# TensorE's first two steps ahead of its loop, the order check on ScalarE, and other orders in the front and the tail of a graph layer

## What is computed

```python
x = x + layer(relu(layernorm(x)), edge_attr_48)

def layer(nodes, edges):
    agg = segment_sum(edges, dst, num_segments=12500)
    u = graph_globals[batch]                  # batch is all 0
    h = concatenate([nodes, agg, u], axis=1)
    return relu(h @ W1 + b1) @ W2 + b2        # W1: 240x256, W2: 256x128
```

## Time and profile before

| | before |
|---|---|
| median of 3 runs (lowest, highest) | 264.44 us (264.34, 265.47) |
| the profiled execution: its time | 264.3 us |
| its span in the profile | 262.5 us |
| mean granted clock of TensorE | 0.978 |
| TensorE busy | 241.3 us, 92% |
| VectorE busy | 229.8 us, 88% |
| ScalarE busy | 144.2 us, 55% |
| POOL busy | 104.9 us, 40% |
| moved by DMA | 94.49 MB, mean 360 GB/s |

### The profile page before, as it was taken

The page is one execution under the profiler, slowest core; times in us unless marked ns, Lnnn a source line. Parts: engine busy times, 40 slices in busy tenths (PEclk is TensorE's granted clock), DMA queues, the critical chain, the costliest instruction groups (busy, mean ns, idle before and its releaser), DMA issues.

```text
span 262.5 us, 17352 instructions
## 1 busy us (share of the span) xinstructions
PE 241.3 (92%) x7438; PEld 197.2 (75%) x7438; DVE 229.8 (88%) x555; ACT 144.2 (55%) x315; POOL 104.9 (40%) x113
## 2 busy tenths in 40 slices
PE   6719799999898999999999999999999999999994
PEld 3517677878777877877987887887897788789753
DVE  2899978999999999999999999999899999997362
...
GB/s 238 372 373 282 391 348 353 379 367 367 345 376 346 332 385 367 355 375 381 382 382 380 381 370 385 373 370 377 376 363 363 368 369 379 382 379 363 403 402 118
DMA packets 70874, 94.49 MB, mean 360 GB/s; under 512 B 4324, under 2 KB 64260, under 8 KB 70854
## 3 DMA queue, kind: packets, MB, share of 16 engines
...
q10 hardware_dynamic: 956, 0.00, 0.2%
...
q0 software_dynamic: 96, 0.00, 0.0%
...
## 4 chain that ended last, share of the span: by engine, by line
PE 59%; DVE 15%; DMA 15%; issue 7%; ACT 3%; DVEq 1%; ACTq 0%
PE group_bank L1063 21%; DMA edge_buf<-in_edge_attr 13%; PE out_bank L1129 12%; PE hidden_bank L1112 10%; PE window_bank L1085 5%; DVE onehot L816 4%; PE out_bank L1102 4%; PE hidden_bank L1116 3%; PE hidden_bank L1118 3%; ACT agg L679 2%; DVE bn L861 2%; DVE out_own L770 2%; DVE agg L845 2%; DVE placing L828 1%; DMA dst_rows<-in_dst 1%
## 5 line engine op out<-in xcount | busy, mean ns | idle before, releaser
L816 DVE TENSOR_TENSOR onehot<-rel,const_bank 128x896 f32<-128x896 f32 (+1 forms) x122 | 122.9, 1023 | 6.1 <-issue 6.0
L1063 PE MATMUL group_bank<-edge_buf,onehot 128*32 128x48 f32 x6454 | 87.2, 211 | 2.9 <-DVE onehot L816 1.4
L1063 PEld LDWEIGHTS group_bank<-edge_buf,onehot 128*32 128x32 f32 x6454 | 79.9, 113 | 8.9 <-issue 4.3
L549 POOL TENSOR_TENSOR tile_sums<-agg,tile_sums 48x512 fp32r<-48x512 f32 x23 | 29.2, 1268 | 130.6 <-ACT tile_sums L642 130.6
L1129 PE MATMUL out_bank<-w_sb,hidden 128*128 128x128 f32 x384 | 48.5, 279 | 1.7 <-issue 0.9
L1129 PEld LDWEIGHTS out_bank<-w_sb,hidden 128*128 128x128 f32 x384 | 44.7, 191 | 4.1 <-issue 1.6
L1112 PE MATMUL hidden_bank<-normed_t,w_node 128*128 128x512 f32 (+1 forms) x100 | 46.5, 588 | 0.4 <-ACT hidden L652 0.4
L620 ACT ACTIVATE normed_x<-x_buf,shift,inverse 128x128 f32<-128x128 f32 x98 | 40.3, 493 | 4.8 <-DVE shift L876 4.8
L652 ACT ACTIVATE hidden<-hidden_bank,hidden_bias 128x512 f32<-128x512 f32 (+1 forms) x50 | 31.2, 676 | 10.6 <-PE hidden_bank L1118 10.6
L528 POOL TENSOR_TENSOR xb_buf<-x_buf,b_rows 128x512 f32<-128x512 f32 (+1 forms) x25 | 31.5, 1262 | 7.3 <-DMA x_buf<-in_x 4.0
L612 ACT ACTIVATE deviation<-mean_var,eps_col 128x4 f32<-128x4 f32 (+1 forms) x25 | 7.4, 298 | 48.0 <-DVE mean_var L867 48.0
...
## 6 DMA issues: line engine op xcount, KB each, us to landing
...
```

The source lines that it names most:

```text
L549: pool.tensor_tensor(sums_tile(k, STACK_LOW), agg_tile(k), sums_tile(k, 0).bitcast(fp32), ALU.subtract)\
L816: dve.tensor_tensor(onehot[:, c0:c0 + cols, :], rel[:, r0:r0 + cols].unsqueeze(2).to_broadcast([P, cols, WINDOW]), ramp_const.unsqueeze(1) ...
L1063: done = pe.matmul(group_bank[h][WINDOW * j:WINDOW * (j + 1), n * F_EDGE:(n + 1) * F_EDGE], onehot[:, (g0 + j) * EDGES_PER_ROW + r, :], ed ...
```

## The change

1. TensorE: steps 0 and 1 are written out ahead of the loop, which now runs from step 2 with one branch in it (`turn_rel`, for steps 2 to 4).
2. The order check: `check_sorted` on VectorE goes. ScalarE's `check_row` takes its place, eight calls in steps 4 to 11, one in each, between `copy_sums(s, 1)` and `deviate`: it copies the first (or last) column of a block of `dst` and sums the positive parts of first minus element (or element minus last). `check_windows` waits for them, and POOL's addition into slot 14 waits for eight instead of four.
3. The front: VectorE's calls up to step 1 are in another order, and POOL makes the places ahead of both zeroings of `agg` instead of between them.
4. The tail: TensorE, ScalarE in another order; `first_layer` is cut into `node_layer` and `sums_layer`, and the last tile has `window_bank` for its hidden values.
5. SP waits for the flag and loads it ahead of its waits for the stores instead of behind them; the instructions are the same.

```diff
@@ -131,7 +131,9 @@
         worst_all = sb("worst_all", [1, 1])
-        violation = sb("violation", [P, blocks + 1])
+        violation = sb("violation", [P, 2 * blocks + 1])
+        row_first = sb("row_first", [P, blocks])
+        row_last = sb("row_last", [P, blocks])
         worst = sb("worst", [P, 1])
@@ -423,12 +426,11 @@
             store_last(last_tile(), last_stored)
+            sp.wait_ge(flag_ready, 1)
+            flag = sp.value_load(general_flag[0:1, 0:1], min_val=0, max_val=1)
             for n in range(OUT_SLOTS):
...
             sp.wait_ge(last_stored, 16)
-
-            sp.wait_ge(flag_ready, 1)
-            flag = sp.value_load(general_flag[0:1, 0:1], min_val=0, max_val=1)
             with sp.If(flag > 0):
@@ -512,9 +514,9 @@
                 pool.memset(tile_sums[p][:, :].bitcast(fp32), 0.0).then_inc(stacks_zeroed, 1)
-            pool.memset(agg[:, 0, :], 0.0).then_inc(agg_zeroed, 1)
             places()
-            pool.memset(agg[:, 1, :], 0.0).then_inc(agg_zeroed, 1)
+            for j in range(2):
+                pool.memset(agg[:, j, :], 0.0).then_inc(agg_zeroed, 1)
@@ -533,7 +535,7 @@
                 if k.static and k.value == OWN_SLOTS - 2:
-                    pool.wait_ge(order_checked, blocks)
+                    pool.wait_ge(order_checked, 2 * blocks)
                 if k.static and k.value == OWN_SLOTS:
@@ -584,6 +586,20 @@
+            def check_row(b, late):
+
+                rows = min(P, n_groups - b * P)
+                act.wait_ge(dst_in[b], 16 * ((b * P < first_last) + 3 * (b == blocks - 1)))
+                n = 2 * b + late
+                ends, col, sign = (row_last, group_edges - 1, -1.0) if late else (row_first, 0, 1.0)
+                act.activation(ends[0:rows, b:b + 1], dst_rows[0:rows, b, col:col + 1], ACT.Copy, scale=sign)\
+                   .then_inc(row_ends_ready, 1)
+                act.wait_ge(row_ends_ready, n + 1)
+                act.activation(order_dump[0:rows, 0:group_edges], dst_rows[0:rows, b, 0:group_edges], ACT.Relu,
+                               bias=ends[0:rows, b:b + 1], scale=-sign, accum_out=violation[0:rows, n:n + 1])\
+                   .then_inc(order_checked, 1)
+                act.wait_ge(order_checked, n + 1)
+
             def copy_rel(b):
@@ -641,7 +657,7 @@
-            def relu_hidden(k):
+            def relu_hidden(k, banks=hidden_bank):
                 if isinstance(k, Again):
@@ -649,7 +665,7 @@
                     cols = strips_of(k) * P
-                    act.activation(hidden[own(k)][:, c, 0:cols], hidden_bank[c][:, 0:cols], ACT.Relu,
+                    act.activation(hidden[own(k)][:, c, 0:cols], banks[c][:, 0:cols], ACT.Relu,
                                    bias=hidden_bias[:, c:c + 1]).then_inc(hidden_copied, 1)
@@ -716,6 +732,8 @@
                 copy_sums(At(s), 1)
+                if 0 <= s - blocks < 2 * blocks:
+                    check_row((s - blocks) // 2, (s - blocks) % 2)
                 deviate(following)
@@ -726,12 +744,12 @@
             copy_sums(At(steps - 1), 0)
+            copy_turned(last, group_bank[1])
+            tile_high(second)
             copy_out(third)
-            tile_high(second)
-            copy_turned(last, group_bank[1])
             tile_high(last)
             relu_hidden(second)
-            relu_hidden(last)
+            relu_hidden(last, window_bank)
             act.wait_ge(flag_ready, 1)
@@ -763,15 +781,6 @@
                    .then_inc(rel_ready, 1)
-
-            def check_sorted(b):
-                rows = min(P, n_groups - b * P)
-                dve.wait_ge(dst_in[b], 16 * ((b * P < first_last) + 3 * (b == blocks - 1)))
-                dve.tensor_tensor_reduce(
-                    out=order_dump[0:rows, 0:group_edges], in0=dst_rows[0:rows, b, 0:group_edges],
-                    in1=dst_rows[0:rows, b, 1:], scale=1.0, scalar=-1.0, op0=ALU.subtract, op1=ALU.max,
-                    accum_out=violation[0:rows, b:b + 1]).then_inc(order_checked, 1)
-                dve.wait_ge(order_checked, b + 1)
@@ -801,7 +810,8 @@
                                        group_live[:, :].unsqueeze(1).to_broadcast([steps, 6, GROUPS]), ALU.mult))
-                link(dve.tensor_reduce(violation[0:steps, blocks:], tests[:, :, :].rearrange("s a g -> s (a g)"),
+                dve.wait_ge(order_checked, 2 * blocks)
+                link(dve.tensor_reduce(violation[0:steps, 2 * blocks:], tests[:, :, :].rearrange("s a g -> s (a g)"),
                                        AX.X, ALU.max))
@@ -901,35 +911,33 @@
             dve.wait_ge(rel_ready, 2)
-            for q in (0, 1, 2):
-                make_onehot(At(0), q)
+            make_onehot(At(0), 0)
             part_bases()
-            for q in (3, 4):
+            for q in (1, 2, 3, 4):
                 make_onehot(At(0), q)
             low_sums(At(0), 0)
-            make_onehot(At(1), 0)
-            moments(At(0))
-            join_moments(At(0))
-            step_bases()
             dve.wait_ge(position_turned, 1)
...
             make_placing(At(0), 0)
+            moments(At(0))
+            join_moments(At(0))
             make_placing(At(0), 1)
+            make_onehot(At(1), 0)
+            invert(At(0))
+            low_sums(At(0), 1)
             make_onehot(At(1), 1)
+            step_bases()
+            make_onehot(At(1), 2)
             base = [window_base(At(0), h) for h in range(2)]
-            invert(At(0))
-            make_onehot(At(1), 2)
             dve.wait_ge(agg_zeroed, 4)
...
             make_placing(At(1), 0)
-            low_sums(At(0), 1)
             make_onehot(At(1), 3)
...
             invert(At(1))
-            check_steps = [2 + b for b in range(blocks)]
             for s in range(1, full_steps):
@@ -959,8 +967,6 @@
                     link(dve.memset(rel[0:masked_rows + 1, c0:c0 + masked_rest], -1.0))
-                if s in check_steps:
-                    check_sorted(check_steps.index(s))
             second, last = At(tiles - 2), last_tile()
@@ -1102,21 +1108,29 @@
-            def first_layer(k):
+            def node_layer(k, banks=hidden_bank):
                 pe.wait_ge(w1_split, 1)
...
                 for c in range(2):
-                    pe.wait_ge(hidden_copied, k.value * 2 + c + 5)
-                    pe.matmul(hidden_bank[c][:, 0:cols], w1_node[:, c * P:(c + 1) * P], normed_t[own(k)][:, 0:cols],
+                    if banks is hidden_bank:
+                        pe.wait_ge(hidden_copied, k.value * 2 + c + 5)
+                    pe.matmul(banks[c][:, 0:cols], w1_node[:, c * P:(c + 1) * P], normed_t[own(k)][:, 0:cols],
                               start=True, stop=False)
+
+            def sums_layer(k, banks=hidden_bank):
                 pe.wait_ge(tile_low_ready, k.value + 3)
+                cols = strips_of(k) * P
                 for c in range(2):
-                    pe.matmul(hidden_bank[c][:, 0:cols], w1_high[:, c * P:(c + 1) * P], tile_sums[own(k)][:, 0:cols],
+                    pe.matmul(banks[c][:, 0:cols], w1_high[:, c * P:(c + 1) * P], tile_sums[own(k)][:, 0:cols],
                               start=False, stop=False)
-                    pe.matmul(hidden_bank[c][:, 0:cols], w1_low[:, c * P:(c + 1) * P], tile_sums[own(k)][:, 0:cols],
+                    pe.matmul(banks[c][:, 0:cols], w1_low[:, c * P:(c + 1) * P], tile_sums[own(k)][:, 0:cols],
                               start=False, stop=True).then_inc(hidden_ready, 1)
+
+            def first_layer(k):
+                node_layer(k)
+                sums_layer(k)
@@ -1159,35 +1173,42 @@
             keep_clock(4, window_bank[0])
-            with pe.Fori(0, full_steps) as i:
+            sum_part(At(0), 0)
+            turn_places()
+            place(At(0), 0)
+            sum_part(At(0), 1)
+            turn_x(At(0))
+            place(At(0), 1)
+            sum_part(At(1), 0)
+            sum_bias()
+            place(At(1), 0)
+            sum_part(At(1), 1)
+            turn_x(At(1))
+            first_layer(At(0))
+            place(At(1), 1)
+            with pe.Fori(2, full_steps) as i:
                 step = At(0, i)
                 sum_part(step, 0)
-                with pe.If(i > blocks):
-                    second_layer(step.plus(-2))
-                with pe.Else():
-                    with pe.If(i > 1):
-                        second_layer(step.plus(-2))
-                        turn_rel(i - 1)
-                    with pe.Else():
-                        with pe.If(i > 0):
-                            sum_bias()
-                        with pe.Else():
-                            turn_places()
+                second_layer(step.plus(-2))
+                with pe.If(i <= blocks):
+                    turn_rel(i - 1)
                 place(step, 0)
...
                 turn_x(step)
-                with pe.If(i > 0):
-                    pe.wait_ge(rel_ready, i * 2)
-                    first_layer(step.plus(-1))
+                pe.wait_ge(rel_ready, i * 2)
```

(12 more changed lines are left out.)

1 line of the change is left out of this document (added).

## The result

| | before | after |
|---|---|---|
| median (lowest, highest) | 264.73 us (264.34, 265.47) | 268.55 us (267.76, 270.75) |
| ratio after/before, 95% interval | | 1.0151 (1.0118 to 1.0185) |
| the profiled execution: its time, span | 264.3, 262.5 us | 269.3, 267.2 us |
| mean granted clock of TensorE | 0.978 | 0.966 |

What follows compares the result with a forecast made beforehand. It took VectorE to bound the early steps, TensorE or the transfers the late ones. Front +0.6, check -3.4, transfers +0.9, tail -0.1 and flag -0.75 summed to -2.75: 261.7 us from the median 264.44, range 259.9 to 264.4.

Steps and rivals of the forecast that it cites:

- TensorE written out: TensorE's steps 0 and 1 ahead of the loop: losing the branches, one of 3.219 us, was costed at nothing.
- The prediction's own sign of being wrong: The forecast is wrong if a TensorE stall of about 3 us stands after 28 us.
- the code itself: Slower rival: TensorE waits for code twice on the path, 3.219 us each, +6.4, 268.1 us; chance 0.06.
- The cover: In the front, VectorE's gapless work up to `step_bases` at 18.2 hides TensorE's late `turn_places`, so its 3.219 us branch costs nothing.
- The check: Order check moved to ScalarE: steps 2 to 4 -1.1, steps 5 and 6 -2.3, sum -3.4; transfers take back +0.9.
- the floor of 10.07: TensorE's least time per step in steps 2 to 4: 9.21 plus 0.86 us for `turn_rel`.
- The look's 1.5 us: Each ScalarE order-check look takes about 1.5 us, hidden in its 1.99 us wait for VectorE's means before `deviate`.
- The front: VectorE's new order up to step 1: +0.6 us in sum, range -1.0 to +2.5, with `step_bases` at -1.97.
- The tail: New order of the last tiles' work at the kernel's end: -0.1 us together, range -0.4 to +0.5.
- The flag: SP's flag load at the end runs while the last store is on its way: -0.75 us, at worst 0.

## Why the prediction was wrong, point by point

- **TensorE written out: the step that failed.** It was costed at "nothing", with "VectorE's sum is the cover". Measured alone: +5.1 us. I took the 3.219 us at line 1168 for a property of a taken branch, which the change removes. It was a wait for code that had not been run before (a packet of code moves in it), it needs no branch, and written-out steps have more of that: 9 packets instead of 4. That code run in a straight line would be there in time was believed from a rule, with no row behind it. The prediction's own sign of being wrong came, a stall of about 3 us after 28 us: 3.50 at 39.31. The kernel before goes through its new code while TensorE mostly waits for VectorE.
- **The rival that came true** was "the code itself", 268.1 us at a chance of 0.06; the median is 268.55. Its mechanism is the right one, though the parts are others: one wait of 3.50 on the path instead of two (that of step 1 doesn't show beside TensorE's wait for VectorE), 1.5 us of low clock behind it, and a later front. That its 268.1 lies so near is luck: by the same sum one such wait gives 264.9. The chance was far too small.
- **The cover**: "I cost it at nothing" for the late `turn_places` was right for the kernel before, and the run with the loop of before shows what it costs once the cover is gone: VectorE's wait of 4.81 us.
- **The check**: -3.4 and +0.9 were forecast, so -2.5; measured alone -2.1 (interval -1.2 to -2.9). The sum came out near, by two errors that cancel: the -1.1 in steps 2 to 4 did not come, since the floor of 10.07 was too low (steps 3 and 4 took (73.41 - 52.96) / 2 = 10.2 each even in the kernel after), and the transfers took nothing back, steps 9 to 20 of the kernel after ran at 9.38. The look's 1.5 us (1.4 measured) and its cover were right.
- **The front**: +0.6 was forecast, 2.4 was measured at the placing of step 1, worth 0.8 (medians) to 1.5 (ratios) in the time with the written-out steps. In the loop the same front costs 5.9 (268.74 against 262.8), mostly by the wait of 4.81 for the turned places. The step mis-sized is `step_bases`: -0.93 instead of -1.97, as its third instruction met POOL's next addition; and the 0.64 of the register loads was not counted at all.
- **The tail**: -0.1 was forecast, +0.8 was measured. The working saw that the window check comes after `tile_low(last)`, but not that `tile_low(last)` itself would come 2.6 us later, behind `copy_out(third)` and beside POOL's addition; the check then ends after TensorE's products for `second` and holds the output.
- **The flag**: -0.75 forecast, 0.9 measured. Right.

Summed in the order check, written-out steps, front, tail, flag: -2.1 + 5.1 + 1.5 + 0.8 - 0.9 = +4.4; measured +4.0 (1.51% of 264.73). Only the first two were run alone, and in another order the front and the written-out steps would have other prices.
